# Second cross-attention on one core: the value and sum products as 512-column blocks, each behind a score of its own

## The chip, the cores and the metric

The kernel runs on one core of one Trainium2 chip. The metric is the device time of one execution in microseconds (us). All tensors of the computation stay the same in the change; only the order of TensorE's instructions in one stage, and the width of some of them, differ.

## What is computed

The reference is two decoder layers with gated residuals, over x of shape (4, 512, 512) and a context of shape (4, 1601, 512). The change lies in the cross-attention of the second layer:

```
q = qkv.reshape(bs * N_HEADS, ch, length)          # layernorm(x), 16 heads of 32 channels
k = v = y.reshape(bs * N_HEADS, ch, -1)            # the context, 1601 columns
weight = einsum('bct,bcs->bts', q * scale, k * scale)
weight = softmax(weight, axis=-1)
a = einsum('bts,bcs->bct', weight, v)
x = x + tanh(g_xattn[1]) * a
```

So for each of 4 x 16 heads a 512 x 1601 matrix of weights is made, normalized over its rows and multiplied by the values. Before it run the first cross-attention and a quantized feed-forward, behind it a second feed-forward.

## The kernel before

The function `cross_attention_1` works on 16 groups (G = 16), each of four heads of 32 channels. What is done for one group's weights is called a slot. The 1601 keys are cut into 13 chunks (MC = 13) of 128, the last of 65.

**Scores and exponentials.** For each chunk c and head h, `score` (L1533) is one fp16 matmul of 512 columns into one of two PSUM buffers, c_scores. ScalarE turns it into weights with an exponential (L1477), written to c_prob, a ring of 4 chunks (RING = 4). The score two further on waits until the exponential has read the buffer. The first exponential of a chunk waits until the chunk four before it has been used.

**Values and sums.** `out` (L1548) multiplies the weights of a chunk, as four fp32 matmuls for the four heads beside each other in the array, by the values, and accumulates in PSUM in c_out. The softmax's denominators are sums over the weights. GpSimd adds up the chunks 0, 1, 2, 3, 5, 6, 8 and 9 (POOLED) in SBUF, in seven additions (L1322); TensorE multiplies that sum by ones (`den_of_sum`, L1571), and the other five chunks (SUMMED: 4, 7, 10, 11, 12) directly (`den`, L1561), all into c_den. VectorE takes the reciprocal in four parts (`finish`, L1403).

**Maxima.** The shift of the softmax is a maximum over the high halves of the scores. These are computed apart: a pair (`pair`, L1516) is two fp16 matmuls of 402 columns into one of two PSUM buffers (c_unit), which VectorE reduces (L1384) before the buffer is written again. A group has 32 pairs. In slot g TensorE issues pairs 16 to 31 of group g+1 and pairs 0 to 15 of group g+2, and a transposition of the maxima (`rows`, L1524). VectorE has, among these reductions, the four reciprocals (before the units of index 3, 4, 5 and 6 of the slot, which are pairs 19 to 22) and the moments of a later group (before pair 0).

**ScalarE's other work** stands at set places: `take_out` before the exponentials of chunk 1, `split_queries` (L1453, L1458) behind those of chunk 1, and `split_keys` (L1445, L1447) behind those of chunk 2.

**The order on TensorE.** A slot is a list of 52 scores, numbered 4 to 55 (4 c + h; 52 to 55 are chunk 0 of the next slot), and what stands behind a score and before the next is called its gap. `placed` says which blocks of products stand in which gap. Pairs are then dealt out by a planner with costs (HALF, PAIR): a pair is given in a gap as long as what has been done so far lies under an even share of the total:

```
upto = (gap - 3) * per_gap
while given < len(stream) and (done + PAIR / 2 <= upto or gap == 4 * MC + 3):
```

Of the kernel before, what the change touches and what calls it, by code (L numbers as in the profile page):

```python
# [16 lines left out]
P = 128  # L17
B, S, D = 4, 512, 512
# [3 lines left out]
MC = (M + P - 1) // P  # L22
ML = M - (MC - 1) * P
# [1053 lines left out]
def cross_attention_1(nc, shared, keys_dram, values_dram, weights_dram):  # L1077
# [3 lines left out]
    with ExitStack() as stack:  # L1081
        def sb(name, shape, dt=F32):
            return stack.enter_context(nc.sbuf_tensor(name, shape, dt))

        def ps(name, shape):
            return stack.enter_context(nc.psum_tensor(name, shape, F32))

        def sem(name):
            return stack.enter_context(nc.semaphore(name))

        H, CH = 4, 32
# [8 lines left out]
        RING = 4  # L1100
        POOLED = [0, 1, 2, 3, 5, 6, 8, 9]
        NP = len(POOLED)
        EXPS, CHUNKS = H * MC, MC
        SUMMED = [c for c in range(MC) if c not in POOLED]
        TURN = 4
        PAIRS = H * TB * 2
        UNITS = PAIRS + 1
# [11 lines left out]
        VT = [sb(f"c_VT{j}", [P, MC, P]) for j in range(2)]  # L1119
        prob = [sb(f"c_prob{j}", [P, H, D]) for j in range(RING)]  # L1120
        psum4 = sb("c_prob_sum", [P, H, D])
        ones32 = sb("c_ones", [P, CH])
# [15 lines left out]
        O = ps("c_out", [P, D])  # L1138
        DEN = ps("c_den", [P, D])
# [20 lines left out]
        exp_done = sem("c_exp_done")  # L1160
        pv_done = sem("c_pv_done")
        out_done = sem("c_out_done")
        den_done = sem("c_den_done")
        sums_taken = sem("c_sums_taken")
# [8 lines left out]
        EXPS0, PV0, UNITS0, FULL0, SCORES0 = 2, RING, 2, 1, 1  # L1173

        def wait(eng, signal, value):
            if not isinstance(value, int) or value > 0:
                eng.wait_ge(signal, value)
# [12 lines left out]
        def turn(n, j):  # L1190
            return n * 8 + 16 - 8 * j
# [309 lines left out]
        def _(pe):  # L1501
# [30 lines left out]
                pe.wait_ge(exp_done, g * EXPS + H * c + h + 1)  # L1532
                nc.tensor.matmul(STp[h % 2][0:w, :], K[p][:, h, c * P:c * P + w], Q[p][:, h, :], start=True, stop=True).then_inc(scores_ready, 1)  # L1533

            WHOLE = 2

            def columns(half):
                return slice(0, D) if half == WHOLE else slice(half * D // 2, (half + 1) * D // 2)

            def out(g, j, c, half):  # L1540
                w, cols = P if c < MC - 1 else ML, columns(half)
                if c == 0:
                    pe.wait_ge(v_loaded[j % 2], 2 * turn(g, j % 2))
                    wait(pe, out_taken, g)
                if half != 1:
                    pe.wait_ge(exp_done, EXPS0 + g * EXPS + H * (c + 1))
                for h in range(H):
                    last = nc.tensor.matmul(O[h * CH:(h + 1) * CH, cols], VT[j % 2][0:w, c, h * CH:(h + 1) * CH],  # L1548
                                            prob[(j * MC + c) % RING][0:w, h, cols], start=c == 0, stop=c == MC - 1 and half == 1)
                if half > 0:  # L1550
                    if c == MC - 1:
                        last.then_inc(out_done, 1)
                    elif c not in SUMMED:
                        last.then_inc(pv_done, 1)

            def den(g, j, c, half):
                w, cols = P if c < MC - 1 else ML, columns(half)
                if c == SUMMED[0]:
                    wait(pe, rden_ready, PARTS * g)
                for h in range(H):  # L1560
                    last = nc.tensor.matmul(DEN[h * CH:(h + 1) * CH, cols], ones32[0:w, :], prob[(j * MC + c) % RING][0:w, h, cols],  # L1561
                                            start=c == SUMMED[0], stop=False)
                if half > 0:
                    last.then_inc(pv_done, 1)

            def den_of_sum(g, half):
                cols = columns(half)
                if half == 0:
                    pe.wait_ge(sums_taken, (g + 1) * NP)
                for h in range(H):  # L1570
                    last = nc.tensor.matmul(DEN[h * CH:(h + 1) * CH, cols], ones32[:], psum4[:, h, cols], start=False, stop=half == 1)  # L1571
                if half == 1:
                    last.then_inc(den_done, 1)

            def last_sums(g, j, i):
                if i < 2:
                    den(g, j, MC - 1, i)
                else:
                    den_of_sum(g, i - 2)

            def placed(before):

                gaps = {}
                for c in range(1, MC):
                    for b in {1: [], 2: [0], 3: [1, 2]}.get(c, [c - 1]):
                        at = 4 * c + (1 if b == c - 1 else 0)
                        if b == 0:
                            gaps.setdefault(at + 1, []).append(("out", b, WHOLE))
                            continue
                        gaps.setdefault(at, []).append(("out", b, 0))  # L1590
                        gaps.setdefault(at + (2 if b not in SUMMED else 1), []).append(("out", b, 1))
                        if b == SUMMED[0]:
                            gaps.setdefault(at + 2, []).append(("den", b, WHOLE))
                        elif b in SUMMED:
                            gaps.setdefault(at + 2, []).append(("den", b, 0))
                            gaps.setdefault(at + 3, []).append(("den", b, 1))
                for half in range(2):
                    gaps.setdefault(4 * MC + 1 + half, []).append(("out", MC - 1, half))
                if before:
                    for i in range(4):  # L1600
                        gaps.setdefault(4 + i, []).append(("last", None, i))
                return gaps

            def slot(g, j, main, nxt, more, later):
                stream = unit_stream(g, j, main, nxt, more)
                if not main:
                    for unit in stream:
                        rows(unit) if unit[0] == "rows" else pair(unit)
                    pe.wait_ge(consts_ready, 7)
                    for h in range(H):  # L1610
                        score(0, 0, 0, h)
                    return
                before = not isinstance(g, int) or g > 0
                gaps = placed(before)
                HALF, PAIR = 0.53, 0.36
                weights = {gap: sum(HALF * (1 + (what != "last" and half == WHOLE)) for what, b, half in parts) for gap, parts in gaps.items()}
                per_gap = (sum(weights.values()) + PAIR * max(len(stream), UNITS)) / (H * MC)
                given, done = 0, 0.0

                def products(gap):  # L1620
                    nonlocal given, done
                    for what, b, half in gaps.get(gap, []):
                        if what == "out":
                            out(g, j, b, half)
                        elif what == "den":
                            den(g, j, b, half)
                        else:
                            last_sums(g - 1, (j - 1) % TURN, half)
                        done += HALF * (1 + (what != "last" and half == WHOLE))
                    upto = (gap - 3) * per_gap  # L1630
                    while given < len(stream) and (done + PAIR / 2 <= upto or gap == 4 * MC + 3):
                        unit = stream[given]
                        if unit[0] == "rows" and gap < ROWS_GAP:
                            break
                        rows(unit) if unit[0] == "rows" else pair(unit)
                        given += 1
                        done += PAIR

                ROWS_GAP = 4 + round((AHEAD + ROWS_AT) * H * MC / UNITS)
                for c in range(1, MC + 1):  # L1640
                    for h in range(H):
                        if c < MC:
                            score(g, j, c, h)
                        elif nxt:
                            score(g + 1, j + 1, 0, h)
                        products(4 * c + h)
                if not nxt:
                    for i in range(4):
                        last_sums(g, j, i)
                assert given == len(stream), (given, len(stream))  # L1650

            every_slot(pe, slot)


# [301 lines left out]
```

## Time and profile before

| | us |
|---|---|
| median of 3 runs | 1890.65 |
| lowest and highest | 1889.88, 1894.62 |
| the profiled execution, its own time | 1892.8 |
| its span | 1891.0 |
| the stage of the change: first score of chunk 1 of group 0 to TensorE's last product | 750 to 1611 |

In the profile PE is TensorE's matmuls, DVE is VectorE, ACT ScalarE and POOL GpSimd. A matmul's row gives the time until its result is out; since they are pipelined, what it costs the engine is read from the start of one row to the start of the next. The fp32 matmuls appear twice in the counts: a block of four heads is x8. PEclk is the clock that TensorE was granted, as a share of 2.4 GHz; it has two levels, 1.2 and 2.4 GHz.

### The profile page before, as it was taken

The page shows a single profiled execution, that of the slowest core. Times are in us where ns is not written, and L with a number is a line of the kernel's source. Part 1 is how long each engine was busy: PE and PEld are TensorE (multiplying, and loading weights), DVE is VectorE, ACT ScalarE, POOL GpSimd, SP SyncE. Part 2 cuts the span into 40 slices and gives each one's busy share as a digit, 9 for nine tenths or more (in the row PEclk, how much of TensorE's full clock was granted, in tenths as well). Part 3 has the DMA queues.
Part 4 walks back from the last instruction along what each step waited for, and adds up shares of the span by engine and source line. Part 5 has one row for each costly group of instructions (what it writes and reads, how often), then busy time and mean ns, then how long its engine had stood idle before and what let it go on. Part 6 is the DMA issues. An engine that isn't in the chain of part 4 may idle for free. (4 is left out here: it accounts for less than half of the span.)

```text
span 1891.0 us, 26498 instructions
## 1 busy us (share of the span) xinstructions
PE 1677.1 (89%) x9744; PEld 658.1 (35%) x9744; DVE 1180.9 (62%) x1538; ACT 860.8 (46%) x1241; POOL 826.1 (44%) x324
## 2 busy tenths in 40 slices
PE   5999999797778877899999999899999999699898
PEld 2444444443333331222222222222222222344443
DVE  3878999884455547766666666566666650534543
ACT  1321211211544332677777677677767778111111
POOL 0022242443221124766767786566878778100000
PEclk9999999899899995999999999899999999799999
DMA  9341222313111123122221222221212224000000
GB/s 329 82 120 50 81 97 87 103 34 123 52 30 34 34 61 90 55 73 73 73 54 50 59 59 73 74 73 43 55 56 67 56 53 93 1 0 22 22 23 23
DMA packets 136413, 124.64 MB, mean 66 GB/s; under 512 B 61775, under 2 KB 112227, under 8 KB 136295
## 3 DMA queue, kind: packets, MB, share of 16 engines
q1 hardware_dynamic: 131302, 112.56, 21.2%
q10 hardware_dynamic: 4992, 10.49, 1.7%
q8 instruction: 77, 1.26, 0.3%
q14 instruction: 42, 0.34, 0.1%
HBM read 73.49 MB, written 10.76 MB: 45 GB/s over the span
## 5 line engine op out<-in xcount | busy, mean ns | idle before, releaser
L1477 ACT ACTIVATE c_prob<-c_scores,ctx_scales 128x512 f32<-128x512 f32 (+1 forms) x832 | 549.8, 686 | 267.7 <-PE c_scores L1533 241.3
L1384 DVE TENSOR_REDUCE c_piece_max<-c_unit 128x1 f32<-128x804 f32 x512 | 486.0, 987 | 277.7 <-PE c_unit L1516 272.1
L1322 POOL TENSOR_TENSOR c_prob_sum<-c_prob_sum,c_prob 128x2048 f32<-128x2048 f32 x96 | 435.0, 4531 | 18.8 <-ACT c_prob L1477 11.5
L1533 PE MATMUL c_scores<-c_queries,c_keys 97*128 97x512 f16 (+1 forms) x832 | 325.7, 397 | 47.4 <-ACT c_prob L1477 39.6
L1516 PE MATMUL c_unit<-c_khigh,c_qdiag 128*128 128x402 f16 x1024 | 267.5, 357 | 35.6 <-DVE c_piece_max L1384 17.8
L1548 PE MATMUL c_out<-c_prob,c_VT 128*32 128x256 f32 (+2 forms) x3200 | 270.0, 410 | 0.0
L676 PE MATMUL a_S<-a_ctxT,a_xnT 128*128 128x401 f32 x512 | 190.2, 516 | 7.2 <-ACT a_prob L633 3.9
L706 PE MATMUL a_o<-a_ctx,a_probT 128*128 128x512 f32 (+1 forms) x416 | 183.5, 598 | 0.0
L1533 PEld LDWEIGHTS c_scores<-c_queries,c_keys 97*128 97x128 f16 (+1 forms) x832 | 80.9, 99 | 285.6 <-ACT c_prob L1477 131.2
L1516 PEld LDWEIGHTS c_unit<-c_khigh,c_qdiag 128*128 128x128 f16 x1024 | 80.1, 100 | 189.2 <-DVE c_piece_max L1384 92.5
L567 ACT COPY a_probT<-a_tp 128x512 f32<-128x512 f32 x48 | 28.0, 586 | 224.5 <-PE a_tp L691 217.5
L1322 POOL TENSOR_TENSOR c_prob_sum<-c_prob 128x2048 f32<-128x2048 f32 x16 | 72.6, 4540 | 131.1 <-ACT c_prob L1477 117.7
L676 PEld LDWEIGHTS a_S<-a_ctxT,a_xnT 128*128 128x128 f32 x512 | 95.7, 196 | 74.9 <-issue 16.7
L1813 ACT ACTIVATE d_silu<-d_u 128x512 f32<-128x512 f32 x44 | 26.3, 597 | 207.6 <-PE d_u L1837 207.6
L706 PEld LDWEIGHTS a_o<-a_ctx,a_probT 128*128 128x128 f32 (+1 forms) x416 | 78.8, 193 | 93.3 <-issue 93.3
L1548 PEld LDWEIGHTS c_out<-c_prob,c_VT 128*32 128x32 f32 (+1 forms) x3200 | 63.9, 109 | 131.6 <-issue 112.2
L358 POOL TENSOR_TENSOR a_weights<-a_picked,a_deq 128x2816 bf16<-128x2816 bf16 x6 | 29.4, 4893 | 178.4 <-DVEq L457 178.4
L1766 DVE SCALAR_TENSOR_TENSOR d_hid<-d_silu,d_hscale,d_u 128x512 f32<-128x512 f32 x44 | 32.8, 746 | 118.5 <-ACT d_silu L1813 118.5
L1561 PE MATMUL c_den<-c_prob,c_ones 128*32 128x256 f32 (+2 forms) x1152 | 99.5, 418 | 0.0
L1837 PE MATMUL d_u<-d_xhi,turned_weights 128*128 128x512 f16 x352 | 91.9, 384 | 5.7 <-DVE d_xlo L1757 5.7
L1837 PE MATMUL d_u<-d_xlo,turned_weights 128*128 128x512 f16 x352 | 90.9, 381 | 0.0
L1403 DVE RECIPROCAL c_rden<-c_den 128x128 f32<-128x128 f32 x64 | 59.8, 941 | 47.8 <-PE c_den L1571 47.8
(197 smaller groups left out, 1974.5 us busy)
## 6 DMA issues: line engine op xcount, KB each, us to landing
c_k<-in_keys SPq DMA_DIRECT2D x16, 801.0 KB, 6.9
c_keys<-c_khigh SPq DMA_DIRECT2D x128, 100.1 KB, 2.2
a_ctx<-in_ctx SPq DMA_DIRECT2D x12, 1024.0 KB, 6.4
c_VT<-in_values SPq DMA_DIRECT2D x16, 768.0 KB
a_ctxT<-in_ctxT SPq DMA_DIRECT2D x12, 802.0 KB, 4.7
c_keys<-c_krest SPq DMA_DIRECT2D x64, 100.1 KB, 2.2
a_weights<-in_L_ffn_weight SPq DMA_DIRECT2D x3, 1408.0 KB, 14.3
weights_back<-a_weights SPq DMA_DIRECT2D x3, 1408.0 KB, 9.7
```

The source lines that it names most:

```text
L676: last = nc.tensor.matmul(S4[:, n, 0:PIECE], xnT[:, d, t * P:(t + 1) * P], CT[:, d, cols], start=d == 0, stop=False)
L706: last = nc.tensor.matmul(O[k % 2][:], probT[0:w, c, :], C[0:w, c, :], start=c == 0, stop=c == MC - 1)
L1322: nc.gpsimd.tensor_tensor(psum4[:], a[:], prob[(j * MC + c) % RING][:], ALU.add).then_inc(sums_taken, 2 if i == 1 else 1)
L1384: nc.vector.tensor_reduce(piece_max[j % 2][:, k // 2, k % 2:k % 2 + 1], U[bank(unit)][:, :, 0:PIECE], axis=AX.XY, op=ALU.max).then_inc(uni ...
L1403: nc.vector.reciprocal(rden[:, cols], DEN[:, cols]).then_inc(rden_ready, 1)
L1477: nc.scalar.activation(prob[(j * MC + c) % RING][0:w, h, :], STp[h % 2][0:w, :], ACT.Exp, scale=score_scale[0:w]).then_inc(exp_done, 1)
L1516: last = nc.tensor.matmul(U[bank(unit)][:, e, 0:PIECE], QZ[o][:, h, t * P:(t + 1) * P], khigh[o][:, at:at + PIECE], start=True, stop=True)
L1533: nc.tensor.matmul(STp[h % 2][0:w, :], K[p][:, h, c * P:c * P + w], Q[p][:, h, :], start=True, stop=True).then_inc(scores_ready, 1)
L1548: last = nc.tensor.matmul(O[h * CH:(h + 1) * CH, cols], VT[j % 2][0:w, c, h * CH:(h + 1) * CH], prob[(j * MC + c) % RING][0:w, h, cols], s ...
L1561: last = nc.tensor.matmul(DEN[h * CH:(h + 1) * CH, cols], ones32[0:w, :], prob[(j * MC + c) % RING][0:w, h, cols], start=c == SUMMED[0], s ...
L1766: nc.vector.scalar_tensor_tensor(hid[:], silu[f % 2][:], hscale[:], U[slot(ST + f)][:, 1, :], ALU.mult, ALU.mult).then_inc(unit_read, 1)
L1837: last = nc.tensor.matmul(U[slot(n)][:, k, :], w12T[k][:, c, f * P:(f + 1) * P], xp[part][:, c, :], start=part == 0 and c == 0, stop=part ...
```

## The change

Blocks are always 512 columns wide; before, all but `out` of chunk 0 and `den` of chunk 4 were issued as two halves of 256 columns, in two gaps. A block of `out` stands in the second gap of a chunk (chunks 0 and 1 and 2: see the table), a block of sums behind the fourth score. The planner counts a block at 1.25 in place of 1.06 (two halves), so that a gap with a block gets no pair. The number of matmuls, the columns, and the work of all other engines stay, save that a product in two halves was 8 instructions and is now 4.

```diff
-            def out(g, j, c, half):
-                w, cols = P if c < MC - 1 else ML, columns(half)
+            def out(g, j, c):
+                w = P if c < MC - 1 else ML
...
                 for h in range(H):
-                    last = nc.tensor.matmul(O[h * CH:(h + 1) * CH, cols], VT[j % 2][0:w, c, h * CH:(h + 1) * CH],
-                                            prob[(j * MC + c) % RING][0:w, h, cols], start=c == 0, stop=c == MC - 1 and half == 1)
+                    last = nc.tensor.matmul(O[h * CH:(h + 1) * CH, :], VT[j % 2][0:w, c, h * CH:(h + 1) * CH],
+                                            prob[(j * MC + c) % RING][0:w, h, :], start=c == 0, stop=c == MC - 1)
...
             def placed(before):
                 gaps = {}
-                for c in range(1, MC):
-                    for b in {1: [], 2: [0], 3: [1, 2]}.get(c, [c - 1]):
-                        at = 4 * c + (1 if b == c - 1 else 0)
-                        if b == 0:
-                            gaps.setdefault(at + 1, []).append(("out", b, WHOLE))
-                            continue
-                        gaps.setdefault(at, []).append(("out", b, 0))
-                        gaps.setdefault(at + (2 if b not in SUMMED else 1), []).append(("out", b, 1))
-                        if b == SUMMED[0]:
-                            gaps.setdefault(at + 2, []).append(("den", b, WHOLE))
-                        elif b in SUMMED:
-                            gaps.setdefault(at + 2, []).append(("den", b, 0))
-                            gaps.setdefault(at + 3, []).append(("den", b, 1))
-                for half in range(2):
-                    gaps.setdefault(4 * MC + 1 + half, []).append(("out", MC - 1, half))
+                for c in range(1, MC + 1):
+                    for i, b in enumerate({1: [], 2: [0], 3: [1, 2]}.get(c, [c - 1])):
+                        gaps[4 * c + 1 + 2 * i] = ("out", b)
+                        if b in SUMMED and b < MC - 1:
+                            gaps[4 * c + 3] = ("den", b)
                 if before:
-                    for i in range(4):
-                        gaps.setdefault(4 + i, []).append(("last", None, i))
+                    gaps[5], gaps[7] = ("last den", None), ("den of sum", None)
...
-                HALF, PAIR = 0.53, 0.36
+                BLOCK, PAIR = 1.25, 0.36
```

Worked through, the two lists give these gaps for an ordinary slot (four gaps to a line, "/" between them, "-" for an empty one). O is a block of `out` by its chunk, D one of `den`, S the sum's; a and b are halves, W a whole block; P is a pair by its number.

```
gaps      before                              | after
 4- 7  D12a / D12b / Sa P16 / Sb                  | P16 P17 / D12W / - / SW
 8-11  P17 P18 / O0W / - / P19 P20                | P18 / O0W / - / P19 P20
12-15  O1a / O2a / O1b P21 / O2b                  | P21 P22 / O1W / - / O2W
16-19  P22 P23 / O3a / P24 / O3b P25              | - / O3W / P23 / P24 P25
20-23  P26 / O4a P27 / O4b / D4W                  | P26 P27 / O4W / - / D4W
24-27  - / O5a P28 / P29 / O5b P30                | - / O5W / P28 / P29
28-31  P31 / O6a P0 / P1 / O6b                    | P30 P31 / O6W / P0 / P1 P2
32-35  P2 P3 / O7a / O7b P4 / D7a                 | P3 / O7W / P4 / D7W
36-39  D7b / O8a / P5 P6 / O8b                    | - / O8W / - / P5 P6
40-43  P7 / O9a / ROWS P8 P9 / O9b                | P7 / O9W / ROWS P8 / P9 P10
44-47  P10 P11 / O10a / O10b / D10a P12           | P11 / O10W / P12 / D10W
48-51  D10b / O11a / O11b / D11a P13              | - / O11W / - / D11W
52-55  D11b / O12a / O12b / P14 P15               | P13 / O12W / - / P14 P15
```

## Rows read from the trace of the kernel before

**Rows 1.** The page: busy time, share of the span and instructions of each engine.

```profile
PE 1677.1 (89%) x9744; PEld 658.1 (35%) x9744; DVE 1180.9 (62%) x1538; ACT 860.8 (46%) x1241; POOL 826.1 (44%) x324
```

**Rows 2.** Busy time by stretch: slots 1 to 13, slot 2, slot 6.

```profile
core 0: us, PE busy (x) PEld busy (x) DVE busy (x) ACT busy (x) POOL busy (x), PEclk, DMA share, GB/s
812.07:1522.90 710.83, 660.16 (x5306) 202.24 (x5304) 458.45 (x531) 507.87 (x742) 511.23 (x179) 0.96 0.23 62
867.50:920.27 52.77, 49.10 (x410) 15.14 (x408) 35.29 (x42) 38.91 (x58) 39.38 (x14) 1.00 0.23 62
1083.27:1137.73 54.46, 50.62 (x409) 15.59 (x408) 35.38 (x42) 39.05 (x58) 39.39 (x14) 0.97 0.24 64
```

**Rows 3.** Waits, 760 to 1608 us: in total, times, longest.

```profile
PE c_scores L1533 <- ACT c_prob L1477: 39.0, 42, 2.4
ACT c_prob L1477 <- POOL c_prob_sum L1322: 23.4, 18, 2.2
...
PE c_unit L1516 <- DVE c_piece_max L1384: 11.3, 32, 0.5
```

**Rows 4.** Timeline of PE in slot 6, gaps 20 to 25, full clock.

```profile
1102.25 0.38 PE L1533 MATMUL c_scores<-c_queries,c_keys 97*128 97x512 f16 x1
1102.47 0.51 PE L1516 MATMUL c_unit<-c_khigh,c_qdiag 128*128 128x402 f16 x2
1102.82 0.38 PE L1533 MATMUL c_scores<-c_queries,c_keys 97*128 97x512 f16 x1
...
1104.36 0.64 PE L1548 MATMUL c_out<-c_prob,c_VT 128*32 128x256 f32 x8
1104.93 0.39 PE L1533 MATMUL c_scores<-c_queries,c_keys 97*128 97x512 f16 x1
1105.25 1.06 PE L1561 MATMUL c_den<-c_prob,c_ones 128*32 128x512 f32 x8
1106.25 0.60 PE L1533 MATMUL c_scores<-c_queries,c_keys 97*128 97x512 f16 x2
```

**Rows 5.** Timeline of PE in slot 6: gaps 11, 13 and 14.

```profile
1090.34 0.85 PE L1516 MATMUL c_unit<-c_khigh,c_qdiag 128*128 128x402 f16 x4
...
1092.23 0.64 PE L1548 MATMUL c_out<-c_prob,c_VT 128*32 128x256 f32 x8
1094.95 0.39 PE L1533 MATMUL c_scores<-c_queries,c_keys 97*128 97x512 f16 x1 [2.08 <-ACT c_prob L1477]
```

**Rows 6.** Timeline of ACT beside it: split_keys between exponentials.

```profile
1091.13 1.62 ACT L1445 ACTIVATE c_k<-c_k,ctx_scales 128x1602 f32<-128x1602 f32 x1
1092.78 1.53 ACT L1447 CAST c_khigh<-c_k 128x1602 f16<-128x1602 f32 x1
```

**Rows 7.** Timeline of PE in slot 6, gap 32: two pairs in a row.

```profile
1113.74 0.52 PE L1516 MATMUL c_unit<-c_khigh,c_qdiag 128*128 128x402 f16 x2 [0.45 <-DVE c_piece_max L1384]
1114.71 0.52 PE L1516 MATMUL c_unit<-c_khigh,c_qdiag 128*128 128x402 f16 x2 [0.45 <-DVE c_piece_max L1384]
```

**Rows 8.** Timeline of DVE in slot 6: reductions, reciprocals, moments.

```profile
1090.89 0.99 DVE L1384 TENSOR_REDUCE c_piece_max<-c_unit 128x1 f32<-128x804 f32 x1 [0.19 <-PE c_unit L1516]
1091.80 0.95 DVE L1403 RECIPROCAL c_rden<-c_den 128x128 f32<-128x128 f32 x1
1092.67 0.93 DVE L1384 TENSOR_REDUCE c_piece_max<-c_unit 128x1 f32<-128x804 f32 x1
...
1102.45 2.80 DVE L1384 TENSOR_REDUCE c_piece_max<-c_unit 128x1 f32<-128x804 f32 x3 [0.24 <-PE c_unit L1516]
...
1111.87 0.69 DVE L1366 BATCH_NORM_STATS2 c_stats<-x_resident 128x6 f32 x1
1112.69 1.00 DVE L1384 TENSOR_REDUCE c_piece_max<-c_unit 128x1 f32<-128x804 f32 x1
```

**Rows 9.** Timeline of PE in slot 5 at the low clock: score, half, score.

```profile
1041.72 0.61 PE L1533 MATMUL c_scores<-c_queries,c_keys 97*128 97x512 f16 x1
1042.26 1.08 PE L1548 MATMUL c_out<-c_prob,c_VT 128*32 128x256 f32 x8
1043.27 0.61 PE L1533 MATMUL c_scores<-c_queries,c_keys 97*128 97x512 f16 x1
```

More of the change, by code:

```diff
@@ L1533, in score @@
                 nc.tensor.matmul(STp[h % 2][0:w, :], K[p][:, h, c * P:c * P + w], Q[p][:, h, :], start=True, stop=True).then_inc(scores_ready, 1)
-            WHOLE = 2
-            def columns(half):
-                return slice(0, D) if half == WHOLE else slice(half * D // 2, (half + 1) * D // 2)
-            def out(g, j, c, half):
-                w, cols = P if c < MC - 1 else ML, columns(half)
+            def out(g, j, c):
+                w = P if c < MC - 1 else ML
                 if c == 0:
@@ L1544, in out, with den @@
                     wait(pe, out_taken, g)
-                if half != 1:
-                    pe.wait_ge(exp_done, EXPS0 + g * EXPS + H * (c + 1))
+                pe.wait_ge(exp_done, EXPS0 + g * EXPS + H * (c + 1))
                 for h in range(H):
-                    last = nc.tensor.matmul(O[h * CH:(h + 1) * CH, cols], VT[j % 2][0:w, c, h * CH:(h + 1) * CH],
-                                            prob[(j * MC + c) % RING][0:w, h, cols], start=c == 0, stop=c == MC - 1 and half == 1)
[L1550 to L1557, printed above, removed]
+                    last = nc.tensor.matmul(O[h * CH:(h + 1) * CH, :], VT[j % 2][0:w, c, h * CH:(h + 1) * CH],
+                                            prob[(j * MC + c) % RING][0:w, h, :], start=c == 0, stop=c == MC - 1)
+                if c == MC - 1:
+                    last.then_inc(out_done, 1)
+                elif c not in SUMMED:
+                    last.then_inc(pv_done, 1)
+            def den(g, j, c):
+                w = P if c < MC - 1 else ML
                 if c == SUMMED[0]:
@@ L1560, in den @@
                 for h in range(H):
-                    last = nc.tensor.matmul(DEN[h * CH:(h + 1) * CH, cols], ones32[0:w, :], prob[(j * MC + c) % RING][0:w, h, cols],
+                    last = nc.tensor.matmul(DEN[h * CH:(h + 1) * CH, :], ones32[0:w, :], prob[(j * MC + c) % RING][0:w, h, :],
                                             start=c == SUMMED[0], stop=False)
[L1563 to L1569, printed above, removed]
-                for h in range(H):
-                    last = nc.tensor.matmul(DEN[h * CH:(h + 1) * CH, cols], ones32[:], psum4[:, h, cols], start=False, stop=half == 1)
-                if half == 1:
-                    last.then_inc(den_done, 1)
@@ L1575, in last_sums, with den_of_sum @@
[L1575 to L1579, printed above, removed]
+                last.then_inc(pv_done, 1)
+            def den_of_sum(g):
+                pe.wait_ge(sums_taken, (g + 1) * NP)
+                for h in range(H):
+                    last = nc.tensor.matmul(DEN[h * CH:(h + 1) * CH, :], ones32[:], psum4[:, h, :], start=False, stop=True)
+                last.then_inc(den_done, 1)
@@ L1614, in slot @@
                 gaps = placed(before)
-                HALF, PAIR = 0.53, 0.36
-                weights = {gap: sum(HALF * (1 + (what != "last" and half == WHOLE)) for what, b, half in parts) for gap, parts in gaps.items()}
-                per_gap = (sum(weights.values()) + PAIR * max(len(stream), UNITS)) / (H * MC)
+                BLOCK, PAIR = 1.25, 0.36
+                per_gap = (BLOCK * len(gaps) + PAIR * max(len(stream), UNITS)) / (H * MC)
                 given, done = 0, 0.0
@@ L1621, in products @@
                     nonlocal given, done
[L1622 to L1629, printed above, removed]
+                    what, b = gaps.get(gap, (None, None))
+                    if what == "out":
+                        out(g, j, b)
+                    elif what == "den":
+                        den(g, j, b)
+                    elif what == "last den":
+                        den(g - 1, (j - 1) % TURN, MC - 1)
+                    elif what == "den of sum":
+                        den_of_sum(g - 1)
+                    if what:
+                        done += BLOCK
                     upto = (gap - 3) * per_gap
@@ L1647, in slot @@
                 if not nxt:
-                    for i in range(4):
-                        last_sums(g, j, i)
+                    den(g, j, MC - 1)
+                    den_of_sum(g)
                 assert given == len(stream), (given, len(stream))
```

## The prediction

> **What bounds the kernel now.** I read the page first: TensorE is busy for 89% of the span, the others for 44 to 62% [rows 1]. That says little, because a matmul's row lasts until its result is out. So I went to stretches of the stage. Slots 1 to 13 take 710.83 us, 54.7 each; slot 2, at the full clock throughout, takes 52.77, slot 6, with a granted clock of 0.97, 54.46 [rows 2]. In such a slot DVE, ACT and POOL are busy for 35 to 39 us, so none of them fills it. Next I read TensorE's timeline from start to start, gap by gap [rows 4]: score to pair 0.22 us, a pair 0.35, score to fp32 block 0.31 (0.09 more than to an fp16 matmul), a half 0.57, a whole 1.00. The reader is to see that a row of 0.64 costs 0.57 and one of 0.38 costs 0.22. An ordinary slot of before has 52 scores, 34 halves, 2 wholes, 32 pairs and the transposition (0.44, not among the rows): 52 x 0.22 + 34 x 0.66 + 2 x 1.09 + 32 x 0.35 + 0.44 = 47.7 us. The other 5.1 of slot 2 are waits, and the views of waits and timeline tell which: one of 2.1 us for an exponential that stands behind `split_keys` on ACT [rows 5, 6], and small ones for DVE's reductions, for example twice 0.6 in gap 32 [rows 7]. So TensorE's own order of work bounds the stage, through its content first and through waits for ACT, DVE and, in some slots, POOL's additions [rows 3] second.
>
> **What the change removes.** 34 halves and 2 wholes (24.6 us) become 19 wholes (20.7): content falls by 3.9 us a slot, to 43.8. It comes from two places: a second switch from fp16 to fp32 (0.09) and a half's fixed part (2 x 0.57 - 1.00 = 0.14), 0.23 for each of 17 blocks. The Trainium skill, Perfetto Trace Analysis, section Matmuls, says that larger matmuls are more efficient than smaller ones when possible; rows 4 agree, 1.00 against 1.14, and if that rule settled the case the kernel would fall by the whole saving. That is the second rival.
>
> **What it moves: the pairs.** A block now fills its gap alone, so that the same 32 pairs are dealt into the gaps between, up to four of them over two neighbouring gaps (the table of gaps in the section on the change). Two PSUM buffers stand between TensorE and DVE. DVE's step is 0.91 us back to back (three reductions in 2.80, the last of them 0.98) [rows 8]. A reduction starts 0.55 after its pair's start (1090.34 and 1090.89 [rows 5, 8]), and the buffer is free 1.05 after the reduction's start (1112.69 and 1113.74 [rows 7, 8]). So a pair starts at least 1.60 us after the second one before it, and in a cluster the pace is 0.91, where TensorE needs 0.35. I went through the new order gap by gap with these numbers, DVE's list and ACT's list beside it. As a test I did the same for the order of before: it gives 52.9 us without low clock, against 52.77 measured in slot 2. For the new order the waits are:
> - gap 4: pairs 16 and 17 come behind 14 and 15 of gap 55. Pair 16 is reached 0.35 + 0.35 + 0.22 = 0.92 after pair 14 and waits 0.65; pair 17 then waits 0.56. Sum 1.2.
> - gap 12: pairs 21 and 22 behind 19 and 20. Pair 21 waits 0.68. Pair 22 needs the reduction of pair 20, and before that DVE does pair 19 and a reciprocal (0.91 + 0.95, [rows 8]): 0.55 + 0.91 + 0.95 + 1.05 = 3.46 after pair 19, where TensorE comes after 1.95. Wait 1.51. Sum 2.2. Behind it the wait on `split_keys` is gone: TensorE now reaches the score of gap 14 later than that exponential's end. One wait takes the other's place, at the same price (2.1 before).
> - gaps 19 and 20, pairs 24 to 27: 0.68 + 0.34 + 0.56 = 1.6.
> - gaps 27 and 28, pairs 29 to 31: 1.0.
> - gaps 31 and 32, pairs 1 to 3, the moments (0.69) ahead of them on DVE: 1.5 (1.2 before in slot 6).
> - gap 39/40 0.7, gaps 42 to 44 with the transposed maxima 1.5 (0.8 before).
> - gaps 9 and 10, scores behind `split_queries`: 0.8 (0.5 before).
>
> Together 10.4 us, where before had 5.1: waits grow by 5.3, content falls by 3.9. The slot of 52.9 becomes 54.36 with the full clock, +1.48. POOL's additions, which hold an exponential in slot 2 (0.9 us), then hold none: the last reciprocal comes earlier, with pair 22 moved from gap 16 to 12, and later gaps not much earlier. SP's list is not touched, and what it serves (the queries' last rows, some 5 us after the transposition of gap 42, needed in gap 52) has cover: over 8 us lie between.
>
> **Sum at the full clock.** Slot 0 +0.2, slot 1 +1.2, slots 2 to 12 11 x 1.48 = +16.3, slot 13 +1.3, slot 14 +1.9, slot 15, without pairs, -1.7 (the blocks' saving there is mostly taken by waits for exponentials). That is +19.1 us.
>
> **The clock.** Slots 1 to 13 took 710.8 us, and 13 x 52.9 are 687.7. Of the 23 us between, 2.6 are one halt at the end of slot 7; the other 20.5 come with falls of the granted clock [rows 2]. In slot 6 TensorE had been idle for 2.1 us in one piece before the fall [rows 5]; at the low level (1.2 GHz) a half takes 1.01 from start to start in place of 0.57 [rows 9], a fall costs some 1.6. So 20.5 / 1.6 makes some 13 falls, about one a slot, slot 2 without one; no fall followed the broken idle of gap 32 (two waits of 0.6 with a pair between). In the new order the idle of gap 12 is as long in sum but broken by a pair (0.68, pair, 1.51), so it lies between these two rows. Bounds: as many falls as before (0 us saved) and none (20.5 saved). I take falls in a third of the slots, and the halt and its fall as before: 11.5 saved, as the longer piece alone is 1.5 and the nearer row is the one without a fall. Result: 19.1 - 11.5 = +7.6 us. The Trainium skill, TensorE: Matmul & The Clock Gate, section A second HAM failure mode: psum-queue depth-cycling, says that a kernel whose PE idles briefly and often between groups goes back and forth between the clock levels; by that rule the new order, with twice the waits, would have more falls than before: the third case below.
>
> Against the profiled execution, 1892.8 (span 1891.0 and 1.8 around it), that gives 1900.4; it lies 2.1 above the median. Against the median: **1898 us**, +0.4%. A measurement of this kernel tells about 0.3% (5.7 us) from no change.
>
> **The rivals.**
> 1. Forecast, 0.5: clustered pairs wait for DVE, the clock falls less. 1898, own range 1893 to 1903.
> 2. TensorE is simply the bound and the saving arrives: 16 slots x 3.9 = -62, 1829 us; with half of it kept, 1860. For it: 93% busy in slot 2 [rows 2]. Against it: 0.91 for each reduction, which no wider block changes. It decides if the waits grow by less than 3.9 us a slot, for instance if a reduction's buffer came free 0.2 us earlier in each cluster. 0.08.
> 3. The falls of the clock stay as frequent or multiply, since idle is now spread over seven places: +19 gives 1910, one more fall in every second slot 10 more, 1920. For it: 10.4 us of idle in a slot. Against: no fall behind short waits in slot 6. 0.22.
> 4. The saving in falls and content cancels the waits: falls vanish and the wait of gap 12 hides more of ACT's; 19.1 - 20.5 = -1.4, 1889. 0.2.
>
> **The range.** The unknown terms are the clock (-9 to +11.5 around the forecast) and the width of a whole block: 0.01 us on each of 19 x 16 blocks would be 3 us if no wait took it up. 1888 to 1914 leaves out rival 2 and the upper end of rival 3. Slower by over 0.3%: rival 3 and two thirds of the forecast, 0.56. Within 0.3%: the rest of the forecast and most of rival 4, 0.32. Faster: rival 2 and a little of 4, 0.12.
>
> **What would show it.** In the profile after: 152 fp32 rows a slot in place of 288, start to start 1.31 for a gap with a block; PE waiting for c_piece_max (L1384's new line) for some 8 to 9 us a slot, in gaps 4, 12, 20, 28, 31 and 44; no wait of over 1.6 us for an exponential behind `split_keys`; slots of 54.4 us with the full clock. Wrong if the pairs of gap 12 start without a wait, if slots fall under 52 us, or if the granted clock lies below 0.97 in every slot.

## The result, and the profile after

The changed kernel takes 1897.36 us (median of 9 runs, 1895.59 to 1901.45), the kernel before in the same runs 1891.53 (1889.88 to 1895.94). The ratio is 1.0029, with a 95% interval of 1.0018 to 1.0040: some 5.5 us slower, beyond what the measurement leaves open. The forecast was 1898 in a range of 1888 to 1914.

TensorE's busy share fell, from 89% [rows 1] to 86%, with 7568 matmuls in place of 9744; the trace holds 7540 of them and all 7568 weight loads. No other engine's busy time changed by more than 15.0 us. The page of the changed kernel, busy time and instructions:

```profile
PE 1623.6 (86%) x7540; PEld 608.1 (32%) x7568; DVE 1173.8 (62%) x1538; ACT 845.8 (45%) x1241; POOL 825.6 (44%) x324
```

Busy time by stretch, changed kernel: slots 1 to 13, slot 2 and slot 6, as in [rows 2].

```profile
core 0: us, PE busy (x) PEld busy (x) DVE busy (x) ACT busy (x) POOL busy (x), PEclk, DMA share, GB/s
814.42:1527.53 713.11, 614.37 (x3537) 160.38 (x3536) 451.83 (x531) 495.51 (x741) 510.66 (x179) 0.99 0.23 62
869.48:923.34 53.86, 46.65 (x274) 12.26 (x273) 34.78 (x42) 38.03 (x58) 39.34 (x14) 1.00 0.23 64
1087.85:1142.39 54.54, 46.89 (x274) 12.39 (x273) 34.87 (x42) 38.23 (x58) 39.35 (x14) 1.00 0.23 64
```

Thirteen slots take 2.3 us more (713.1 against 710.8). Slot 2 is 1.1 us longer than before at the same full clock. Slot 6 is as long as before (54.54 against 54.46), but for another reason: its granted clock is 1.00 where it was 0.97. Over all thirteen slots the clock rose from 0.96 to 0.99. So there are two terms of opposite sign, as the forecast had them. The profiled execution's span is 6.2 us longer; 2.6 of these lie ahead of the stage, whose first gap opens at 752.7 us, before at 750.1. Nothing ahead of it was edited, and over the ten kernels profiled here this start lies between 750.0 and 752.7, so they are hardly the change's. The stage itself, to TensorE's last product, grew by 3.9 us, from 861.2 to 865.1.

Waits in the stage of the changed kernel (in total, times, longest), to be set against [rows 3]:

```profile
PE c_unit L1516 <- DVE c_piece_max L1384: 98.4, 208, 1.2
...
PE c_scores L1533 <- ACT c_prob L1477: 13.1, 47, 0.6
```

TensorE's wait for VectorE grew from 11.3 to 98.4 us, in 208 places for 32; its wait for exponentials fell from 39.0 to 13.1, and the longest of them from 2.4 to 0.6. The timeline of slot 6 shows why. PE, gaps 11 to 15:

```profile
1095.92 0.85 PE L1516 MATMUL c_unit<-c_khigh,c_qdiag 128*128 128x402 f16 x4
1096.61 0.38 PE L1533 MATMUL c_scores<-c_queries,c_keys 97*128 97x512 f16 x1
1097.52 0.52 PE L1516 MATMUL c_unit<-c_khigh,c_qdiag 128*128 128x402 f16 x2 [0.53 <-DVE c_piece_max L1384]
1099.23 0.52 PE L1516 MATMUL c_unit<-c_khigh,c_qdiag 128*128 128x402 f16 x2 [1.20 <-DVE c_piece_max L1384]
1099.58 0.38 PE L1533 MATMUL c_scores<-c_queries,c_keys 97*128 97x512 f16 x1
1099.89 1.06 PE L1542 MATMUL c_out<-c_prob,c_VT 128*32 128x512 f32 x8
1100.89 0.61 PE L1533 MATMUL c_scores<-c_queries,c_keys 97*128 97x512 f16 x2
```

And VectorE beside it:

```profile
1096.46 1.00 DVE L1384 TENSOR_REDUCE c_piece_max<-c_unit 128x1 f32<-128x804 f32 x1 [1.02 <-PE c_unit L1516]
1097.38 0.95 DVE L1403 RECIPROCAL c_rden<-c_den 128x128 f32<-128x128 f32 x1
1098.24 0.93 DVE L1384 TENSOR_REDUCE c_piece_max<-c_unit 128x1 f32<-128x804 f32 x1
1099.09 0.94 DVE L1403 RECIPROCAL c_rden<-c_den 128x128 f32<-128x128 f32 x1
```

Pairs 19 and 20 start at 1095.92. Pair 21 starts 0.06 us behind the reduction of pair 19 (1097.46), pair 22 0.06 behind that of pair 20 (1099.17), which itself stood behind a reciprocal. The reader is to see that VectorE has hardly a break from 1096.46 on, while over this whole slot it is busy for 35 of 54.5 us: it is the bound of a cluster, not of the slot. ScalarE's split_keys ends at 1099.89 in this slot:

```profile
1098.36 1.53 ACT L1447 CAST c_khigh<-c_k 128x1602 f16<-128x1602 f32 x1
1099.80 1.26 ACT L1477 ACTIVATE c_prob<-c_scores,ctx_scales 128x512 f32<-128x512 f32 x2
```

and the score of gap 14, at 1100.89, no longer waits for the exponential behind it. (ScalarE's first row is `split_keys`, its second the exponentials behind it.) The clusters of gap 4 and gap 28, PE again:

```profile
1088.71 0.52 PE L1516 MATMUL c_unit<-c_khigh,c_qdiag 128*128 128x402 f16 x2 [0.48 <-DVE c_piece_max L1384]
1089.62 0.52 PE L1516 MATMUL c_unit<-c_khigh,c_qdiag 128*128 128x402 f16 x2 [0.39 <-DVE c_piece_max L1384]
...
1114.15 0.52 PE L1516 MATMUL c_unit<-c_khigh,c_qdiag 128*128 128x402 f16 x2 [0.27 <-DVE c_piece_max L1384]
1115.05 0.52 PE L1516 MATMUL c_unit<-c_khigh,c_qdiag 128*128 128x402 f16 x2 [0.39 <-DVE c_piece_max L1384]
```

The second pair of a cluster follows the first at 0.91 and 0.90 us: that is VectorE's step.

### The profile page after: what moved, and what is told of

It reads as the page before. It is cut to its first block and busy times, and to the rows that moved or that the text cites. A ratio compares the mean times of both kernels' runs of the same rounds, so it can differ in the third digit from the quotient of the medians.

```text
span 1897.2 us, 22118 instructions
## 1 busy us (share of the span) xinstructions
PE 1623.6 (86%) x7540; PEld 608.1 (32%) x7568; DVE 1173.8 (62%) x1538; ACT 845.8 (45%) x1241; POOL 825.6 (44%) x324
## 5 line engine op out<-in xcount | busy, mean ns | idle before, releaser
L1477 ACT ACTIVATE c_prob<-c_scores,ctx_scales 128x512 f32<-128x512 f32 (+1 forms) x832 | 534.6, 685 | 287.4 <-PE c_scores L1533 279.9
L1533 PE MATMUL c_scores<-c_queries,c_keys 97*128 97x512 f16 (+1 forms) x832 | 299.5, 390 | 21.8 <-ACT c_prob L1477 13.7
L1542 PE MATMUL c_out<-c_prob,c_VT 128*32 128x512 f32 (+1 forms) x1664 | 224.5, 612 | 0.1
L1533 PEld LDWEIGHTS c_scores<-c_queries,c_keys 97*128 97x128 f16 (+1 forms) x832 | 74.4, 98 | 335.4 <-ACT c_prob L1477 290.3
L1554 PE MATMUL c_den<-c_prob,c_ones 128*32 128x512 f32 (+1 forms) x640 | 86.1, 610 | 0.0
L433 DVE TENSOR_SCALAR a_level<-a_weights 128x2816 bf16<-128x2816 bf16 x78 | 77.3, 1030 | 1.2
```

The costliest lines, as they stand in the source:

```text
L433: return nc.vector.tensor_scalar(out[:], x, at, NF4[to], test, ALU.mult)
L1477: nc.scalar.activation(prob[(j * MC + c) % RING][0:w, h, :], STp[h % 2][0:w, :], ACT.Exp, scale=score_scale[0:w]).then_inc(exp_done, 1)
L1542: last = nc.tensor.matmul(O[h * CH:(h + 1) * CH, :], VT[j % 2][0:w, c, h * CH:(h + 1) * CH], prob[(j * MC + c) % RING][0:w, h, :], start=c ...
L1554: last = nc.tensor.matmul(DEN[h * CH:(h + 1) * CH, :], ones32[0:w, :], prob[(j * MC + c) % RING][0:w, h, :], start=c == SUMMED[0], stop=False)
```

## The experiments

The theory: a slot's time is the content of TensorE's list plus its waits, and the change trades 3.9 us of content for some 5 us of waits that pairs in clusters make for VectorE; falls of the clock come from the long unbroken wait behind split_keys. The rivals: the wide blocks themselves hold the scores back so that ScalarE runs dry; the pairs are hidden work; the clock has nothing to do with it. "Slots below 1.00" counts those of slots 1 to 13 whose granted clock was below 1.00. Ratios are to the kernel before, from runs beside it on the same chip.

| | median us | ratio (95%) | slots 1 to 13, us | clock there | slots below 1.00 |
|---|---|---|---|---|---|
| kernel before | 1891.53 | 1 | 710.8 | 0.96 | 11 |
| changed kernel | 1897.36 | 1.0029 (1.0018 to 1.0040) | 713.1 | 0.99 | 3 |
| e1: wide blocks, pairs as before | 1874.25 | 0.9901 (0.9880 to 0.9922) | 693.3 | 0.97 | 8 |
| e2: halves, pairs as after | 1918.91 | 1.0126 (1.0107 to 1.0146) | 732.6 | 0.99 | 1 |
| e3: changed kernel, block at 0.50 | 1834.44 | 0.9673 (0.9651 to 0.9695) | 656.2 | 0.97 | 9 |
| e4: kernel before with a filler | 1880.22 | 0.9924 (0.9906 to 0.9942) | 697.2 | 0.99 | 2 |
| e5: half the reduction | 1818.06 | 0.9606 (0.9582 to 0.9629) | 647.3 | 0.99 | 1 |
| e6: kernel before, half at 0.25 | 1850.00 | 0.9775 (0.9749 to 0.9801) | 672.0 | 0.98 | 5 |
| e7: a written table | 1801.40 | 0.9517 (0.9493 to 0.9541) | 623.7 | 0.99 | 1 |
| e8: two pairs later | 1906.53 | 1.0074 (1.0047 to 1.0100) | 723.0 | 0.98 | 5 |

### e1: the width alone

The changed kernel's blocks in its gaps, but the planner deals pairs by the list of before (`halves` is the old `placed`):

```diff
-                BLOCK, PAIR = 1.25, 0.36
-                per_gap = (BLOCK * len(gaps) + PAIR * max(len(stream), UNITS)) / (H * MC)
+                HALF, PAIR = 0.53, 0.36
+                weights = {gap: sum(HALF * (1 + (what != "last" and half == WHOLE)) for what, b, half in parts) for gap, parts in halves(before).items()}
+                per_gap = (sum(weights.values()) + PAIR * max(len(stream), UNITS)) / (H * MC)
...
-                    if what:
-                        done += BLOCK
+                    done += weights.get(gap, 0.0)
```

> The changed kernel's blocks of 512 columns in its gaps, but each pair in the gap where the kernel before had it. Theory (clustered pairs wait for VectorE): content stays 43.8 us a slot, the waits of the clusters go, those for exponentials behind split_keys and for the additions come back; slots of 51.7 us at the full clock, falls of the clock in about eight slots, in all some 21 us less than before: 1870 us (1862 to 1878). Rival (the width is to blame: a gap of 1.31 us holds the next score back and ScalarE runs dry): the loss of the change stays, 1893 us or more.

Measured 1874.25, ratio 0.9901: some 19 us less than before. Slots 1 to 13 and slot 2 of e1:

```profile
811.77:1505.11 693.34, 618.52 (x3537) 167.94 (x3535) 455.97 (x531) 494.52 (x742) 511.25 (x179) 0.97 0.24 64
864.53:916.04 51.51, 46.02 (x273) 12.63 (x273) 35.10 (x42) 37.82 (x58) 39.39 (x14) 1.00 0.22 63
```

Slot 2 takes 51.51, 1.3 less than before and 2.3 less than after. The width is a gain, and the rival that blames it falls. But it is a gain of 1.3 where the content fell by 3.9: with 43.8 of content, slot 2 of e1 has 7.7 us of waits where before had 5.1, although every pair stands in its old gap. The shorter list brings the pairs closer together in time, and TensorE meets VectorE more often. The waits of slot 2 in e1 show it (in before this wait is under 0.1 us there, in after 6.5):

```profile
PE c_unit L1516 <- DVE c_piece_max L1384: 2.0, 7, 0.5
```

For exponentials TensorE waits 36.0 us here up to 1500 us, the longest 2.3: that wait is back, and the clock is at 0.97.

### e2: the order of the pairs alone

```diff
-                weights = {gap: sum(HALF * (1 + (what != "last" and half == WHOLE)) for what, b, half in parts) for gap, parts in gaps.items()}
+                weights = {gap: 1.25 for gap in wholes(before)}
...
-                        done += HALF * (1 + (what != "last" and half == WHOLE))
+                    done += weights.get(gap, 0.0)
```

`wholes` is the new `placed`; blocks and their gaps are those of before.

> The kernel before with its halves in their gaps, but the pairs in the gaps where the changed kernel has them. Theory: content stays 47.7 us a slot and the clusters' waits are added almost in full; slots of 55.6 us at the full clock, hardly any fall of the clock: some 26 us more than before, 1917 us (1908 to 1926). Rival (pairs are hidden, the width made the loss): no change, 1888 to 1895 us.

Measured 1918.91, ratio 1.0126, some 24 us more. Slots 1 to 13 and slot 2:

```profile
817.43:1550.00 732.57, 657.66 (x5305) 196.89 (x5304) 454.31 (x531) 506.47 (x741) 510.77 (x179) 0.99 0.23 61
872.56:928.04 55.48, 50.22 (x409) 14.99 (x408) 34.95 (x42) 38.99 (x58) 39.34 (x14) 1.00 0.23 62
```

The order costs 2.7 us in slot 2 (55.48 against 52.77), and it alone raises the clock to 0.99. In slot 2, width and order together give 53.86; from 52.77, e1 takes 1.26 off and e2 puts 2.71 on, which adds up to 54.22, 0.36 more than that. So the two terms are nearly independent: the width is worth 1.3 with the old order and 1.6 with the new.

### e3: one number of the planner

```diff
-                BLOCK, PAIR = 1.25, 0.36
+                BLOCK, PAIR = 0.50, 0.36
```

> The changed kernel with one number changed: the planner counts a block at 0.50 in place of 1.25, so that pairs are dealt nearly evenly over the gaps, also into gaps that hold a block. Theory: the waits for VectorE nearly vanish, the wait behind split_keys comes back as the longest; slots of 49.2 us at the full clock, with a fall of the clock in most of them: some 55 us less than before, 1836 us (1825 to 1848). Rival (a gap with block and pair, 1.66 us, starves ScalarE, which is why none should be there): 1890 us or more.

Measured 1834.44, ratio 0.9673. Slot 2, and TensorE's rows around 1080 us, where pairs and blocks take turns (the two pairs shown start 1.9 us apart):

```profile
859.83:908.78 48.95, 45.28 (x273) 12.59 (x272) 35.55 (x42) 37.54 (x58) 39.40 (x14) 1.00 0.26 70
```
```profile
1079.96 0.51 PE L1516 MATMUL c_unit<-c_khigh,c_qdiag 128*128 128x402 f16 x2
1080.31 0.38 PE L1533 MATMUL c_scores<-c_queries,c_keys 97*128 97x512 f16 x1
1080.62 1.06 PE L1554 MATMUL c_den<-c_prob,c_ones 128*32 128x512 f32 x8
1081.62 0.39 PE L1533 MATMUL c_scores<-c_queries,c_keys 97*128 97x512 f16 x1
1081.85 0.51 PE L1516 MATMUL c_unit<-c_khigh,c_qdiag 128*128 128x402 f16 x2
```

The same matmuls in the same blocks, 3.6% apart from the changed kernel (0.9673 and 1.0029). The planner's 1.25 is near a block's true price of 1.09, but the planner leaves out the scores (0.22 each) and levels TensorE's work from gap to gap, where what had to be levelled is VectorE's.

### e4: filling the wait before the clock falls

```diff
+                    if gap == 13:
+                        for h in range(H):
+                            nc.tensor.matmul(O[h * CH:(h + 1) * CH, :], zeros32[:], prob[(j * MC + 1) % RING][:, h, :], start=False, stop=False)
```

> The kernel before with one more block in gap 13 of each slot: a product of the weights of chunk 1 with zeros, added to the output's sum, which it leaves as it is; it lies in the wait of 2.1 us behind split_keys. Theory of the clock (what it falls after is this idle time, and a fall costs some 1.2 to 1.6 us): slots 1 to 13 lose most of their falls, about 12 us less than before: 1879 us (1874 to 1884), although TensorE does more. Rival (the falls cost nothing that the later waits would not take anyway, or come from elsewhere): no change, or up to 16 x 1.0 us more if the block does not fit into the wait.

Measured 1880.22, ratio 0.9924: 14.4 us less, with 64 more fp32 matmuls a kernel (128 rows, 9872 in place of 9744). PE in gap 13 of slot 6 (with lines shifted by the addition), where the wait is now 1.22 in place of 2.08, and slots 1 to 13:

```profile
1087.04 1.04 PE L1634 MATMUL c_out<-c_prob,c_zeros 128*32 128x512 f32 x8
1089.30 0.39 PE L1535 MATMUL c_scores<-c_queries,c_keys 97*128 97x512 f16 x1 [1.22 <-ACT c_prob L1479]
```
```profile
813.00:1510.16 697.16, 653.79 (x5409) 202.03 (x5408) 457.71 (x531) 505.89 (x742) 511.28 (x179) 0.99 0.24 63
865.77:918.54 52.77, 49.95 (x417) 15.40 (x416) 35.27 (x42) 38.89 (x58) 39.37 (x14) 1.00 0.24 65
```

Slot 2, which had the full clock before, stays at 52.77 to the hundredth: the filler costs nothing where there is no fall. All that is gained, 13.7 us in slots 1 to 13, came with the clock, from 0.96 to 0.99; slot 6 fell from 54.46 to 53.13, so a fall costs 1.3 us there. The change breaks the same wait with a pair, and its clock rises as far.

The wait makes falls likely and does not decide them one by one. The same wait stands in slot 2 of the kernel before, at the full clock:

```profile
879.03 0.39 PE L1533 MATMUL c_scores<-c_queries,c_keys 97*128 97x512 f16 x1 [2.09 <-ACT c_prob L1477]
```

In the changed kernel the wait column has nothing over 1.20 in slots 1 and 3, and yet both have a clock of 0.97. What else decides is not shown here.

### e5: the reduction halved

```diff
-U[bank(unit)][:, :, 0:PIECE], axis=AX.XY
+U[bank(unit)][:, 0:1, 0:PIECE], axis=AX.XY
```

> The changed kernel, with each of VectorE's reductions reading only the first of a pair's two matmuls (402 columns in place of 804), so half of the maxima are left out; TensorE issues all it did. Theory (VectorE's step of 0.91 us sets the clusters' pace): the step falls to about 0.5, the waits in gaps 4, 12, 20, 28, 31, 44 all but go, slots of 49.1 us at the full clock with hardly a fall: some 73 us less than the kernel before, 1818 us (1805 to 1832). Rival (the waits go back to something else in TensorE's order, such as the width of the blocks): 1885 us or more.

Measured 1818.06, ratio 0.9606. The reduction's group and slot 2:

```profile
L1384 DVE TENSOR_REDUCE c_piece_max<-c_unit 128x1 f32<-128x402 f32 x512 | 285.5, 570 | 398.0 <-PE c_unit L1516 385.8 <-DVE c_nrow L1394 2.1
```
```profile
854.47:903.59 49.12, 46.19 (x273) 12.27 (x273) 22.44 (x42) 37.69 (x58) 39.39 (x14) 1.00 0.26 70
```

With TensorE's order exactly that of the changed kernel, 0.41 us off each of 512 reductions takes some 80 us off the kernel (0.9606 against 1.0029). The theory gave 49.1 for a slot. VectorE's step is the cause, and nothing in TensorE's own list.

### e6: the planner's price without the width

```diff
-                HALF, PAIR = 0.53, 0.36
+                HALF, PAIR = 0.25, 0.36
```

> The kernel before, halves and all, with the planner's price of a half at 0.25 in place of 0.53: the same even dealing of pairs as with a block at 0.50, without the wide blocks. Theory: slots of 50.8 us at the full clock; some 37 us less than before, 1854 us (1845 to 1864), so the price alone is worth two thirds of what price and width together are worth (1834 measured), and the width the other 20. Rival (the price does nothing for halves, since their clusters are small): 1885 us or more.

Measured 1850.00, ratio 0.9775, some 42 us less than before. A low price also spreads the pairs of the kernel before; so of e3's 3.3% two thirds come from the price and one third from the width (0.9673 against 0.9775).

### e7: a table for the gaps

```diff
+            OUT_GAPS = [9, 13, 15, 17, 21, 26, 29, 33, 38, 41, 45, 49, 53]
+            DEN_GAPS = {4: 23, 7: 36, 10: 47, 11: 51}
+            UNIT_GAPS = [5, 6, 8, 10, 11, 12, 12, 14, 17, 18, 20, 22, 24, 25, 27, 28, 30, 31, 34, 34, 36, 36, 39, 40, 42, 43, 44, 46, 48, 50, 51, 54, 55]
...
+                    gaps[4], gaps[7] = ("last den", None), ("den of sum", None)
...
-                    while given < len(stream) and (done + PAIR / 2 <= upto or gap == 4 * MC + 3):
+                    table = len(stream) == UNITS
+                    while given < len(stream) and ((gap >= UNIT_GAPS[given]) if table else (done + PAIR / 2 <= upto or gap == 4 * MC + 3)):
```

Where a slot's list has another length, the planner stands, with a block at 0.50.

> Blocks of 512 columns and pairs in gaps written out as a table for an ordinary slot: no gap cluster of more than two pairs, a pair behind the block in several gaps, two pairs in gap 12 to fill TensorE's time while ScalarE is busy with split_keys, sums of chunk 12 in gap 4. Worked through with the steps of the prediction it gives slots of 47.1 us at the full clock, set then by GpSimd's additions and what stands between them, and one or two falls in all: some 93 us less than before, 1799 us (1785 to 1815). Rival (below 49 us ScalarE or the ring of weights holds the scores and the table is no better than a block at 0.50): 1830 us.

Measured 1801.40, ratio 0.9517: the fastest, 4.8% ahead of the kernel before and 5.1% ahead of the changed one. Slots 1 to 13 and slot 2:

```profile
809.58:1433.31 623.73, 590.70 (x3538) 168.60 (x3536) 459.19 (x531) 487.69 (x741) 511.63 (x179) 0.99 0.26 70
856.68:903.79 47.11, 45.03 (x274) 12.95 (x273) 35.31 (x42) 37.36 (x58) 39.42 (x15) 1.00 0.27 73
```

47.11 us where 47.1 was expected. Of these 43.8 are content, so 3.3 us of waits are left. Slots 3, 5, 6, 9 and 11 take up to 48.44: in them a pair waits for a DMA (c_qdiag), 2.9 us in all five and 1.0 at most, which the expectation had not foreseen.

### e8: is the wait of gap 12 an extra one

```diff
+                        if before and len(stream) == UNITS and gap < {5: 14, 6: 16}.get(given, 0):
+                            break
```

> The changed kernel with pairs 21 and 22 in gaps 14 and 16 in place of 12, all else as it was. The prediction said that the wait of gap 12 only takes the place of the one behind split_keys, at the same price. If so: gap 12 loses its 2.2 us, the score of gap 14 waits some 1.7 us for the exponential, slots stay at 54.6 us and the time within 4 us of the changed kernel, 1897 to 1903. Rival (the wait of gap 12 is an extra one): some 1.5 us a slot less, 1875 us.

Measured 1906.53, ratio 1.0074; against the changed kernel some 8 us more (0.0045 of 1891), so above the expected 1897 to 1903. PE, gaps 12 to 14 of slot 6, and slots 1 to 13 and slot 6:

```profile
1097.93 0.65 PE L1533 MATMUL c_scores<-c_queries,c_keys 97*128 97x512 f16 x2
1098.51 1.07 PE L1542 MATMUL c_out<-c_prob,c_VT 128*32 128x512 f32 x8
1101.85 0.39 PE L1533 MATMUL c_scores<-c_queries,c_keys 97*128 97x512 f16 x1 [2.28 <-ACT c_prob L1477]
```
```profile
812.62:1535.61 722.99, 617.62 (x3537) 162.18 (x3536) 455.73 (x531) 495.51 (x741) 511.09 (x179) 0.98 0.23 61
1089.16:1144.04 54.88, 46.69 (x273) 12.45 (x273) 35.17 (x42) 38.15 (x58) 39.41 (x14) 1.00 0.23 63
```

The two waits of gap 12 are gone, and one of 2.3 us for the exponential stands in gap 13's end instead, not 1.7: the rival (1875) falls, the wait was no extra one. But the time is a miss, and slots 1 to 13 are 9.9 us longer than after. Two things make this up. At the full clock a slot is 0.3 longer, 54.88 against 54.54 in slot 6, since one wait of 2.3 takes the place of two that sum to 2.05; over thirteen slots that is near half of the 9.9. The rest stands in the slots with a lowered clock: five lie below 1.00 in place of three. The expectation had no term for them, though the prediction's clock part does. In slot 6 the unbroken 2.28 stands at the full clock: again the wait alone does not make a fall.

## Why the prediction was right

**Content against waits.** Right, and in size. Content was put at 43.8 after 47.7 and waits at 10.4 after 5.1. In slot 2 of the changed kernel the waits, from start to start, sum to 9.9: gap 4 1.2, gap 12 2.1 (forecast 2.2), gaps 19 and 20 1.6, gap 28 1.0, gaps 31 and 32 1.2 (forecast 1.5), gap 40 0.7, gaps 43 and 44 1.6, gaps 9 and 10 0.6 (forecast 0.8). The steps of slot 6: gap 12, pair 21 waits 0.69 (1097.52 - 1096.61 - 0.22; forecast 0.68); pair 22 1.36 (1.71 - 0.35; forecast 1.51, mostly since a reciprocal's step is 0.86 there, not the 0.95 used); gap 4, 0.64 and 0.56 (forecast 0.65 and 0.56). The wait column gives less than that, 0.53 and 1.20 in gap 12, as it counts from the modelled end of the matmul before. e5 shows VectorE's step as the cause, e1 and e2 part the two terms: the width takes 1.3 us off slot 2, the order puts 2.7 on it. So of the 5 us by which waits grew, about half belong to the order and half came with the shorter content under either order, which the prediction did not tell apart.

The additions of GpSimd, which held exponentials for 23.4 us before [rows 3], hold them for 1.7 us after, in two places; that was forecast too.

**One wait in place of the other.** Right: the wait behind split_keys is gone after, and comes back in e8 with a slot that is 0.3 us longer.

**The sum at the full clock.** The slot was put at 54.36, +1.48 over the 52.9 worked out for before. (The parts as printed, 52.9 - 3.9 + 5.3, make 54.3.) Measured: slot 2, 53.86 against 52.77, +1.1; slots 4 to 11, which stand in a loop, 54.54 against 53.13, +1.4. The 53.13 is slot 10 of the kernel before, at the full clock:

```profile
1308.01:1361.14 53.13, 49.16 (x409) 15.32 (x408) 35.28 (x42) 38.91 (x58) 39.40 (x14) 1.00 0.23 62
```

For slots 2 to 12 that makes 3 x 1.1 + 8 x 1.4 = 14.5 where 16.3 was put down, so the +19 for the stage was some 2 us high, and the two kinds of slot were taken as one.

**The clock.** The direction was right, the share too cautious. I took falls in a third of the slots. The granted clock of slots 1 to 13 went from 0.96 to 0.99: 11 slots were below 1.00 before and 3 are after, one of them behind the halt at the end of slot 7. Against this the price was too high, 1.6 for a fall where slot 6 shows 1.3. And the 20.5 us were not all the clock's: they held the loop's longer slots too (8 x 0.36). e4 got 13.7. Had the falls stayed, the change would have cost near 1%.

**The number.** Forecast 1898, measured 1897.36. That it is within 1 us is partly luck. The stage was to grow by 7.6 us and grew by 3.9 in the profiled pair, as the sum at the full clock was some 2 us high and the clock gave back some 2 more; 2.6 us from ahead of the stage filled most of the difference.

**The rivals.** That TensorE's content decides (1829) fell, since the waits for VectorE rose from 11.3 to 98.4 us in this view. The rule of larger matmuls, from the Trainium skill, Perfetto Trace Analysis, section Matmuls, is right by itself, as e1 shows with 1%; it doesn't say what the freed time is filled with. The third rival, that falls stay or multiply, fell as well: three slots below 1.00 for eleven. It is also what the Trainium skill, TensorE: Matmul & The Clock Gate, section A second HAM failure mode: psum-queue depth-cycling, would make of the many short waits. No run bears that out here: the kernels whose many waits are all short (after and e2, both 0.99) have 3 and 1 slots below 1.00, and those with one unbroken wait of 2.1 to 2.3 us (before, e1, e8) have 11, 8 and 5. The fourth, cancelling at -1.4, was too low: the stage's +3.9 lies about midway between it and the forecast's +7.6. The whole kernel's +5.5 lies just under the 5.7 that the prediction took as the least it could tell from no change; nine runs of each told it.

## What to carry to other kernels

When small work items are dealt into the gaps of an engine's list, space them by the step of the engine that consumes them and by the number of buffers between, not by the producer's load: here two buffers and a step of 0.91 us, where the producer needs 0.35. A saving in the producer's content is mostly taken by new waits until the items are spread anew: of 3.9 us in 52.8, 1.3 arrived with the old spacing (e1) and none with the planner's new one. Spread evenly, wide blocks and one number in the planner gave 3.3%, with a table 4.8%. If TensorE must wait long, break the wait with something it can do; even work that is thrown away gave 0.8% (e4).

## What was not expected of the hardware

Slots inside the loop are longer than the same slots written out, at the full clock and with the same list: 54.54 against 53.86 after, 53.13 against 52.77 before, 53.13 against 52.77 in e4. The scores' timeline puts over half of the difference in gap 9 (0.15 us) and in gap 31 or 32 (0.15 to 0.23); what causes it was not tried. And at the end of slot 7, where the loop of slots 4 to 11 starts its second pass, TensorE halts for 2.5 to 3.4 us in all ten kernels (3.3 after), once in the whole stage, with nothing that the profile shows to wait for. In all ten, slot 8, behind it, has a granted clock of 0.88 to 0.97.
